# Linear attention's product on two 64-row halves of the array, and z's first tile split by operand parts, in a fused perceiver block

## What is computed

```
qkv = x @ W_qkv;  q, k, v = split(qkv)
q = relu(rmsnorm(q));  k = relu(rmsnorm(k))          # 16 heads of 32
kv = einsum('bhnd,bhne->bhde', k, v)                  # per head 32 x 32
out = einsum('bhnd,bhde->bhne', q, kv)
normalizer = einsum('bhnd,bhd->bhn', q, k.sum(2)) + eps
out = out / normalizer
return out @ W_out + b_out                            # z in the kernel's names
```

## Time and profile before

| | |
|---|---|
| Time, median of 3 runs | 527.33 us (526.98 to 527.74) |
| The profiled execution | 527.25 us, span of the profile 525.1 us |
| PE busy | 520.9 us, 99% of the span |
| DVE, ACT, POOL busy | 374.2, 243.3, 245.3 us |
| Granted clock of TensorE | 1.00 over the span |

### The profile page before, as it was taken

One profiled execution on the slowest core, in us unless ns is written; L12 is line 12 of the kernel. 1 busy time (PEld: TensorE's weight loads), 2 busy tenths in 40 slices (PEclk: granted clock), 3 DMA queues, 4 the chain that ended last, 5 costly groups with the idle time before them and its releaser, 6 DMA issues.

```text
span 525.1 us, 6996 instructions
## 1 busy us (share of the span) xinstructions
PE 520.9 (99%) x2536; PEld 434.4 (83%) x2536; DVE 374.2 (71%) x615; ACT 243.3 (46%) x391; POOL 245.3 (47%) x159
## 2 busy tenths in 40 slices
PE   9999999999999999999999999999999999999997
PEld 8888888888888888888888888888888888988885
DVE  5673677876667766567878644999967477739996
ACT  4743434745535444453554534656645332562210
POOL 3735006331211322224244243338519948888993
PEclk9999999999999999999999999999999999999999
DMA  8721233232422223322232212242250312751102
GB/s 307 315 70 52 81 85 116 104 137 82 149 92 80 81 92 144 143 104 81 102 139 80 82 40 73 81 169 80 98 183 1 120 42 90 253 200 60 61 1 80
DMA packets 17607, 57.10 MB, mean 109 GB/s; under 512 B 2083, under 2 KB 2595, under 8 KB 16806
## 3 DMA queue, kind: packets, MB, share of 16 engines
q1 hardware_dynamic: 17286, 56.27, 30.5%
q10 hardware_dynamic: 288, 0.39, 0.2%
HBM read 54.55 MB, written 2.10 MB: 108 GB/s over the span
## 4 chain that ended last, share of the span: by engine, by line
PE 99%; DVE 0%; issue 0%; POOL 0%; POOLq 0%
PE bank L1463 28%; PE bank L1581 11%; PE bank L1592 11%; PE bank L1582 11%; PE bank L1594 11%; PE bank L1583 11%; PE bank L1593 11%; PE bank L1513 2%; PE bank L1453 1%; PE bank L1731 1%; PE bank L1474 1%; PE bank L1488 0%; PE bank L1720 0%; PE bank L1782 0%; DVE xs L1444 0%; PE bank L1749 0%
## 5 line engine op out<-in xcount | busy, mean ns | idle before, releaser
L575 POOL TENSOR_TENSOR cn_l<-raw_n,cn_h 128x1024 fp32r<-128x1024 f32 x32 | 77.7, 2428 | 185.5 <-ACT cn_h L757 185.5
L775 ACT COPY ring<-bank 128x512 f32<-128x512 f32 x64 | 37.7, 589 | 148.3 <-PE bank L1583 148.1
L1100 DVE TENSOR_TENSOR top<-top,bank 128x512 f32<-128x512 f32 x60 | 41.1, 685 | 86.4 <-ACT ring L775 86.3
L1581 PE MATMUL bank<-qk_h,ct_h 128*128 128x512 f32 x256 | 99.8, 390 | 0.0
L1583 PE MATMUL bank<-qk_h,ct_l 128*128 128x512 f32 x256 | 99.6, 389 | 0.0
L1582 PE MATMUL bank<-qk_l,ct_h 128*128 128x512 f32 x256 | 99.6, 389 | 0.0
L1592 PE MATMUL bank<-ph,cn_h 128*128 128x512 f32 x256 | 99.6, 389 | 0.0
L1593 PE MATMUL bank<-pl,cn_h 128*128 128x512 f32 x256 | 99.6, 389 | 0.0
L1594 PE MATMUL bank<-ph,cn_l 128*128 128x512 f32 x256 | 99.6, 389 | 0.0
L1581 PEld LDWEIGHTS bank<-qk_h,ct_h 128*128 128x128 f32 x256 | 48.0, 188 | 10.6 <-issue 0.8
L1583 PEld LDWEIGHTS bank<-qk_h,ct_l 128*128 128x128 f32 x256 | 48.1, 188 | 10.1
(11 more groups left out here) (248 smaller groups left out, 911.7 us busy)
## 6 DMA issues: line engine op xcount, KB each, us to landing
raw_t<-ctx_t SPq DMA_DIRECT2D x32, 512.0 KB, 4.2
raw_n<-ctx_n SPq DMA_DIRECT2D x32, 512.0 KB, 3.3
piece_raw<-pieces SPq DMA_DIRECT2D x12, 512.0 KB, 3.4
shifted<-xn_rows SPq DMA_DIRECT2D x12, 256.0 KB, 3.1
taps<-taps_in SPq DMA_DIRECT2D x1, 1280.0 KB, 7.5
xs<-x SPq DMA_DIRECT2D x4, 256.0 KB, 5.6
wq_raw<-wq_t SPq DMA_DIRECT2D x4, 256.0 KB, 6.3
wk_raw<-wk_in SPq DMA_DIRECT2D x1, 1024.0 KB, 7.9
```

The lines of the kernel that those rows point to most:

```text
L575: pool.tensor_tensor(cn[p % CNB][1][:], raw_n[p % 2][:], cn[p % CNB][0][:].bitcast(F32), ALU.subtract).then_inc(cnl_ready, 1)
L1100: dve.tensor_tensor(top[:], top[:], bank[:, S_BANKS[i % 2], :], ALU.max).then_inc(max_done, 1)
L1581: pe.matmul(bank[:, dst, :], ct[i // 2 % 2][0][:, c, keys], qk[0][:, c, :], start=(c == 0), stop=False)
```

## The change

The 16 matmuls of `linear` become 32, each on a 64-row half of the array: rows 0 to 63 (r = 0) hold two heads of a chunk, rows 64 to 127 (r = 1) the other two. Each uses 64 x 128 of `qrT` as weights and streams 66 columns of `kv` (two heads), and the halves write to different banks. The block-diagonal matrix shrinks from 132 to 66 columns a chunk, and DVE makes it for two chunks in one operation. All of `linear` now stands ahead of the first transposes. The first tile of `heads` is signalled once and not in halves. z's first tile is written out by hand in a bank of its own (`Z_BANKS`): the eight products that need only `xT_h` come first, starting once ACT has written it, with the transposes of tile 1 between the first four and the second four; the four products with `xT_l` come last. Other tiles of z only change banks.

```diff
-        kvmask = at(172.5, "kvmask", [P, HG, HW])
+        kvmask = at(172.5, "kvmask", [P, 2, HW])
-        kv = at(168.25, "kv", [P, C, VW])
+        kv = at(168.25, "kv", [P, C, 2 * HW])
-                pool.memset(kvmask[h * DH:(h + 1) * DH, h, :], 1.0).then_inc(masks_ready, 1)
+                pool.memset(kvmask[h * DH:(h + 1) * DH, h % 2, :], 1.0).then_inc(masks_ready, 1)
-        HEAD_BANKS = (2, 3, 0, 1)
+        HEAD_BANKS = (2, 1, 0, 1)
+        Z_BANKS = (3, 2, 0, 1)
# DVE
-            for c in range(C):
-                dve.wait_ge(kv_psum, c + 1)
-                dve.tensor_tensor(kv[:, c, :].rearrange("p (h w) -> p h w", h=HG),
-                                  bank[:, KV_BANKS[c], 0:HW].unsqueeze(1).to_broadcast([P, HG, HW]), kvmask[:],
-                                  ALU.mult).then_inc(kv_ready, 1)
+            for pair in range(2):
+                dve.wait_ge(kv_psum, 2 * pair + 2)
+                at_bank = KV_BANKS[2 * pair]
+                dve.tensor_tensor(kv[:, 2 * pair:2 * pair + 2, :].rearrange("p c (i w) -> p c i w", i=2),
+                                  bank[:, at_bank:at_bank + 2, 0:HW].unsqueeze(2).to_broadcast([P, 2, 2, HW]),
+                                  kvmask[:].unsqueeze(1).to_broadcast([P, 2, 2, HW]), ALU.mult).then_inc(kv_ready, 1)
...
-                for b in range(2):
-                    if t == 0 and b == 1:
-                        ins.then_inc(heads_ready, 1)
+                for r in range(2):
                     ins = dve.tensor_tensor(
-                        heads[:, t, b * 2 * P:(b + 1) * 2 * P].rearrange("p (g h e) -> p g h e", g=2, h=HG),
-                        la[:, b, :, :, 0:DH],
-                        rnorm[:, t, 2 * b:2 * b + 2, :].unsqueeze(3).to_broadcast([P, 2, HG, DH]), ALU.mult)
+                        heads[:, t, :].rearrange("p (c r i e) -> p r c i e", c=C, r=2, i=2)[:, r],
+                        la[:, r, :, :, 0:DH],
+                        rnorm[:, t, :, 2 * r:2 * r + 2].unsqueeze(3).to_broadcast([P, C, 2, DH]), ALU.mult)
...
-                dve.tensor_tensor(xs[:, t, :], xs[:, t, :], bank[:, HEAD_BANKS[t], :], ALU.add).then_inc(x2_ready, 1)
+                dve.tensor_tensor(xs[:, t, :], xs[:, t, :], bank[:, Z_BANKS[t], :], ALU.add).then_inc(x2_ready, 1)
# PE
-            def linear(t, chunks=range(C)):
-                pe.wait_ge(qrT_ready, C)
-                for c in chunks:
-                    if t == 0:
-                        pe.wait_ge(kv_ready, c + 1)
-                    ins = pe.matmul(bank[:, LA_BANKS[t] + c // 2, c % 2 * VW:(c % 2 + 1) * VW],
-                                    qrT[:, c, t * P:(t + 1) * P], kv[:, c, :], start=True, stop=True)
-                if c == C - 1:
-                    ins.then_inc(la_psum, 1)
-            linear(0)
-            linear(1)
-            linear(2, (0, 1))
+            def linear(t):
+                for c in range(C):
+                    if t == 0 and c % 2 == 0:
+                        pe.wait_ge(kv_ready, c // 2 + 1)
+                    for r in range(2):
+                        two = slice(r * 2 * DH, (r + 1) * 2 * DH)
+                        ins = pe.matmul(bank[:, LA_BANKS[t] + r, c * 2 * HW:(c + 1) * 2 * HW],
+                                        qrT[two, c, t * P:(t + 1) * P], kv[two, c, :], start=True, stop=True,
+                                        tile_position=(r * 2 * DH, 0))
+                ins.then_inc(la_psum, 1)
+            pe.wait_ge(qrT_ready, C)
+            for t in range(TT):
+                linear(t)
...
             transpose_heads(0)
-            linear(2, (2, 3))
-            linear(TT - 1)
-            transpose_heads(1)
             pe.wait_ge(w2_ready, 2 * len(W2_ORDER))
-            for t in range(TT):
+            def first_z(c, a, b):
+                return pe.matmul(bank[:, Z_BANKS[0], :], xT[a][:, c, 0:P], wout[b][:, c, :], start=(c == 0 and a == b),
+                                 stop=(c == C - 1 and a == 1))
+            pe.wait_ge(xh_ready, 3 * TT + 1)
+            for c in range(C):
+                if c == 2:
+                    transpose_heads(1)
+                first_z(c, 0, 0)
+                first_z(c, 0, 1)
+            pe.wait_ge(xl_ready, 3 * TT + 1)
+            for c in range(C):
+                ins = first_z(c, 1, 0)
+            ins.then_inc(z_psum, 1)
+            transpose_heads(2)
+            for t in range(1, TT):
                 pe.wait_ge(xl_ready, 3 * TT + t + 1)
...
-                    ins = project(HEAD_BANKS[t], [cut(xT, c, t * P, (t + 1) * P) for c in some],
+                    ins = project(Z_BANKS[t], [cut(xT, c, t * P, (t + 1) * P) for c in some],
```

More of the change, by code:

```diff
@@ L1308, in _ @@
             dve.wait_ge(masks_ready, MASKS)
-            for c in range(C):
-                dve.wait_ge(kv_psum, c + 1)
-                dve.tensor_tensor(kv[:, c, :].rearrange("p (h w) -> p h w", h=HG),
-                                  bank[:, KV_BANKS[c], 0:HW].unsqueeze(1).to_broadcast([P, HG, HW]), kvmask[:],
-                                  ALU.mult).then_inc(kv_ready, 1)
+            for pair in range(2):
[4 more added lines that the diff above has]
+                                  kvmask[:].unsqueeze(1).to_broadcast([P, 2, 2, HW]), ALU.mult).then_inc(kv_ready, 1)
             for t in range(TT):
                 dve.wait_ge(la_psum, t + 1)
-                la = bank[:, LA_BANKS[t]:LA_BANKS[t] + 2, 0:2 * VW].rearrange("p b (g h w) -> p b g h w", g=2, h=HG)
-                dve.tensor_scalar(norm[:, t].rearrange("p (b g) h -> p b g h", b=2), la[:, :, :, :, DH], den_eps[:, t:t + 1], None,
+                la = bank[:, LA_BANKS[t]:LA_BANKS[t] + 2, 0:2 * VW].rearrange("p r (c i w) -> p r c i w", c=C, i=2)
+                dve.tensor_scalar(norm[:, t].rearrange("p c (r i) -> p r c i", r=2), la[:, :, :, :, DH], den_eps[:, t:t + 1], None,
                                   ALU.add).then_inc(norm_ready, 1)
@@ L1724, in _ @@
                             ins.then_inc(kv_psum, 1)
-            def linear(t, chunks=range(C)):
-                pe.wait_ge(qrT_ready, C)
-                for c in chunks:
-                    if t == 0:
-                        pe.wait_ge(kv_ready, c + 1)
-                    ins = pe.matmul(bank[:, LA_BANKS[t] + c // 2, c % 2 * VW:(c % 2 + 1) * VW],
-                                    qrT[:, c, t * P:(t + 1) * P], kv[:, c, :], start=True, stop=True)
-                if c == C - 1:
-                    ins.then_inc(la_psum, 1)
-            linear(0)
-            linear(1)
-            linear(2, (0, 1))
-            def transpose_heads(t):
[L1742 to L1750, removed]
+            def linear(t):
[11 more added lines that the diff above has]
+                linear(t)
+            def transpose_heads(t):
+                pe.wait_ge(heads_ready, t + 1)
+                transpose_tile(heads, t, HEAD_BANKS[t]).then_inc(xnT_psum, 1)
             def transpose_x2(t):
```

## The result

The changed kernel takes 528.29 us, the median of 22 executions (527.80 to 530.25), against 527.22 us for the kernel before in the same comparison. The ratio is 1.0028, 95% interval 1.0022 to 1.0034: slower by 1.2 to 1.8 us. The forecast was 528.4. Three executions far above the rest, 1068.97 and 654.01 us of the kernel before and 881.55 us of one experiment's kernel (the last two at a mean granted clock of 0.75 and 0.56), are left out of every ratio and mean here.

The account below looks back on a forecast made before the run. PE, busy 99% of the span, was taken to bound the kernel; -0.11 + 0.17 + 0.10 - 0.05 + 0.94 + 0.01 = +1.06 us on 527.33 gave 528.4 us. Its own range was 528.1 to 528.8, over the cases 526.9 to 530.0.

Parts of the forecast that it names:

- linear on halves, with the wait for the matrix: Linear's 64 half-array records save 0.11 us; its second half waits for the block-diagonal matrix from DVE, +0.17 us.
- second change of mode, less the old wait for heads: Going from halves to full-array transposes after linear costs +0.10 us; transposes of tile 0 no longer wait for heads, -0.05 us.
- the wait for ACT, with z in two pieces: PE idles before z's first tile until ACT writes the high part, +0.94 us; one more change of operand, +0.01 us.
- The load binds, not the stream: In linear on halves, each record takes its 128-column weight load, 109 ns, not its 66-column stream of 55 ns.
- The matrix in pairs: DVE's block-diagonal matrix operation for two chunks has 264 elements, 0.43 us; PE's wait for the second costs +0.17 us.
- Halves side by side: In linear, the two row halves run concurrently, each with its own chain of load and stream, as column parts do.
- loads in turns: Rival: linear's halves share one weight path, 212 ns a pair; z's first tile 4.1 us late, 531.4 us; chance 0.08.
- no load ahead: Rival: in linear a half can't load ahead of its own stream; +2.6 us, 530.0 us; chance 0.07.
- Nothing given back: After z's first tile PE runs without a gap; the +1.06 us carries to the end, nothing added or recovered.
- The fast halves: Rival: in linear a half's load takes half the time or hides, 57.5 ns a record; 527.1 us; chance 0.10.
- The clock: Rival: clock falls in PE's new wait or under half-filled rows; z's first tile costs 2.1 us more, 530.5+; chance 0.05.

Follow-up runs that it names:

- The blocks: Changed kernel with extra float32 matmul blocks behind its last matmul, on the full array or row parts, results unused, in three kernels; 128-column loads 109 to 112 ns at full clock.
- the gap-covered kernel: Changed kernel with linear on the full array, and linear of tile 3 and transposes of tile 1 ahead of the wait for ACT; 527.07 us, ratio 0.9998.
- halves alone: Changed kernel with PE's order of before and z in one piece in the transposes' banks, linear still on halves; 527.50 us, stage +0.52 us against before.
- gap part filled: Changed kernel with the transposes of tile 1 moved ahead of the wait for ACT; 528.05 us, stage +0.64 us against before.
- z in one: Changed kernel with transposes of tile 1 ahead of the wait and z's first tile not split by parts; 528.42 us, stage +1.31 us against before.
- order-alone: Changed kernel with linear back on the full array and the 132-column matrix in four operations; 527.68 us, stage +0.98 us against before.
- the first kernel with blocks: Changed kernel plus seven matmul blocks on the full array, halves, one half and quarters; 112 ns a record, two halves with 132 columns 188 ns a pair.
- the third of these kernels: Changed kernel plus four blocks on both halves, each entered from six matmuls on the first half alone; some 112 ns a pair in all four.

## Why the prediction was right, and where its terms were off

By its own steps, in the terms of the chain:

| step | forecast, us | measured, us |
|---|---|---|
| linear on halves, with the wait for the matrix | -0.11 + 0.17 = +0.06 | 3.78 - 3.80 = -0.02 |
| second change of mode, less the old wait for heads | +0.10 - 0.05 = +0.05 | (0.60 + 0.44) - (0.49 + 0.44) = +0.11 |
| the wait for ACT, with z in two pieces | +0.94 + 0.01 = +0.95 | 0.75 + (1.18 + 1.84 - 2.75) = +1.02 |
| sum | +1.06 | +1.11 |

*The load binds, not the stream: right.* The forecast rested on one record of 380 ns among those of 276. The blocks show it without the rest: 112 ns a load of 128 columns down to a stream of 33. The size was off by 3 ns, 112 instead of 109, so the 32 periods gain 0.02 us and not 0.11. Linear before sat on both limits at once, load 112 and stream 112.5.

*The entry: a term that the sum didn't have.* The first record on halves lasts 322 ns where the others last 272, 50 more, against 380 - 276 = 104 before: going into linear costs some 0.05 us less.

*The matrix in pairs: a wrong count.* I priced an operation of 264 elements; it has 2 x 66 = 132, takes 0.30 us as before, and the load that waits for it (435.51 + 0.30) stands at 435.86, so that some 0.05 us are lost instead of 0.17. The three together, +0.09, -0.05 and -0.12, are the -0.08 between forecast and measurement in the table's first row.

*Halves side by side: right*, argued from column parts and now shown on row parts. With it two of the slow rivals fall, loads in turns and no load ahead.

*The change of mode: right in place, 0.05 short*: 0.60 against 0.45 for the transposes, with linear on halves and on the full array, where +0.10 was forecast.

*The wait for ACT: right in place, 0.06 short.* ACT ends at 439.83 + 0.59 = 440.42 and the load starts at 440.53:

```profile
440.53 0.19 PEld L1754 LDWEIGHTS bank<-w_out_h,xT_h 128*128 128x128 f32 x1 [0.98 <-issue]
```

0.11 us from ACT to PE, where I had taken the 0.05 of DVE to PE.

*Nothing given back: right*, by the 78.63 and 78.62 us behind the stage. That the gap is the loss is shown best by the gap-covered kernel: with the same parts of z and the same banks, but linear on the full array and the gap closed, the loss is gone. Halves with the gap fully closed and z by parts were not run; halves alone comes nearest to it, at +0.52.

*The fast halves*, the rival on the other side, needed a load of half the time for half the rows. The Trainium skill, "TensorE: Matmul & The Clock Gate", section "LDWEIGHTS (loading the stationary operand)", says that the rows don't count; the blocks agree, 112 ns on 32, 64 and 128 rows, and 58 ns at 64 columns. *The clock* stayed: the granted clock was 1.00 in and behind the gap, and no block of matmuls behind it is slower (z of tile 1 takes 2.77 us in both kernels). The rival was no idle one, though: behind a block on one half alone the clock did fall to 0.50 for 3.4 us in one execution. Its price was read from records near 5 us, where the column says 1.00; the trace's clock records begin only at 6.32 us, so that 1.00 is no measurement. Whether those records ran at 0.50 isn't shown.

The agreement of the sum, +1.06 and +1.11, is in part luck: linear came out 0.08 lower, and the change of mode and the wait for ACT 0.06 and 0.07 higher. The chances: 0.53 for slower was a fair reading of a sum that lay on the bound. The ratio came out above that bound, at 1.0028. The medians alone differ by 1.07 us (1.0020), as the stage does; the means differ by 1.37 us (528.60 and 527.23), since the changed kernel has some executions 2 us long, told of below. So part of the measured ratio is not the stage's, and that it came out above the bound, not on it, is luck too.

## What to carry to other kernels

Splitting a product over row parts of the array divides what is streamed, not what is loaded: each part still pays for all columns of its weights. Before such a split, compare load and stream of one matmul; here they were equal, so there was nothing to win, and each block on parts costs some 0.15 us to leave. When work is moved ahead of a hand-over to other engines, add up what it covered where it stood: 0.9 us of linear and 0.44 of transposes hid a way of 1.0 us over ACT, and moving them without removing anything made that way visible. And when one block in a trace is slow, read its granted clock before looking for a cause in the kernel: 188 ns a pair was a mean of 220 at 0.50 and 112 at 1.00.

## What was not expected

Ten of the 51 executions of the kernels with linear on halves (changed, halves alone, gap part filled, z in one) took over 529 us, up to 2.5 us above their medians. Of the 22 executions of the two kernels with the new order on the full array none did, nor did any of the 65 of the kernel before. Two of the ten were profiled. In the changed kernel's (530.21 us) the time lies in the last store's landing, 4.3 us instead of 2.1. In the one of z in one (529.14 us) that store landed after 2.1 us and the span is 526.3 us, so what is extra lies outside the profiled span. Eight of the ten have long spans, as the first has (527.1 to 528.2 us), and two have not (526.2 and 526.3); for the eight of the ten that have no trace, where the time lies is not known. Whether halves have to do with it isn't shown.

A semaphore from ACT reached PE's next load after 0.11 us, with the full array and with halves alike (the order-alone chain has the same 0.14 us of issue), twice what DVE's takes.

The granted clock fell to 0.50 once while PE was at work: at 530.40 us of the first kernel with blocks, after 2.7 us on one half of the array alone, and it was back at 1.00 at 533.82. What brought the clock down isn't shown: in the third of these kernels four shorter blocks on one half left it at 1.00, and so did 3.8 us of linear on both halves in the changed kernel.
